# Attention's last batches and the second routing in another order, and the second pair's loads directly behind the first's

## The reference

```
x = x + 0.5 * ffn(layernorm(x))
x = x + attention(layernorm(x))      # 16 heads of 16 channels, softmax over 256 keys
x = x + 0.5 * ffn(layernorm(x))
```

## Time and profile before

| | us |
|---|---|
| median of 3 runs | 862.64 (858.92 to 864.11) |
| the profiled execution | 856.83 |
| its span, first to last instruction | 855.1 |
| TensorE busy | 729.3 (85%) |
| VectorE busy | 602.2 (70%) |
| ScalarE busy | 432.6 (51%) |
| POOL busy | 458.0 (54%) |
| mean granted TensorE clock | 0.957 of full |

### The profile page before, as it was taken

One profiled execution on the slowest core, in us unless ns is written; L12 is line 12 of the kernel. 1 busy time (PEld: TensorE's weight loads), 2 busy tenths in 40 slices (PEclk: granted clock), 3 DMA queues, 4 the chain that ended last, 5 costly groups with the idle time before them and its releaser, 6 DMA issues.

```text
span 855.1 us, 17528 instructions
## 1 busy us (share of the span) xinstructions
PE 729.3 (85%) x4774; PEld 568.2 (66%) x4774; DVE 602.2 (70%) x1435; ACT 432.6 (51%) x922; POOL 458.0 (54%) x446
## 2 busy tenths in 40 slices
PE   1775649999999997789999889787499999999984
PEld 1443326788888886667766667555268888888872
DVE  4775737777777776477787577457387777777766
ACT  3655324555555555257656455454325555555551
POOL 6876723666666667433344342146516666666672
PEclk9999999999999999999999798689689999999998
DMA  8998878868888753544453223027555787887766
GB/s 303 347 388 333 314 238 319 282 217 281 266 284 294 242 192 117 188 158 162 148 184 120 92 106 121 34 68 262 201 162 184 252 256 258 268 268 242 228 229 227
DMA packets 87419, 188.87 MB, mean 221 GB/s; under 512 B 13072, under 2 KB 37920, under 8 KB 85792
## 3 DMA queue, kind: packets, MB, share of 16 engines
q1 hardware_dynamic: 47104, 106.07, 36.4%
q10 hardware_dynamic: 26448, 41.92, 14.8%
q0 software_dynamic: 13776, 39.75, 12.2%
HBM read 105.46 MB, written 65.45 MB: 200 GB/s over the span
## 4 chain that ended last, share of the span: by engine, by line
PE 35%; DVE 13%; another core or an unknown queue 4%; issue 3%; ACT 2%; POOL 1%; DMA 0%; SPq 0%; DVEq 0%; ACTq 0%
PE s_psT L945 12%; PE s_psG L969 6%; DVE s_a_nm L1732 4%; PE s_psO L1499 3%; PE s_psS L1464 2%; PE s_psS L926 2%; PE s_psS L912 2%; PE s_psG L1436 2%; PE s_psT L1480 1%; DVE all_x L2188 1%; PE s_psT L1484 1%; PE s_psR L1571 1%; PE s_psG L1449 1%; PE s_psG L1522 1%
## 5 line engine op out<-in xcount | busy, mean ns | idle before, releaser
L1357 POOL DMA_INDIRECT rows<-s_a_row,s_a_slot_i x64 | 62.4, 975 | 107.6 <-DVE s_a_slot_i L1860 88.9
L1132 POOL DMA_INDIRECT kbuf<-s_e_own_ys,s_e_own_place x79 | 80.9, 1024 | 66.3 <-ACT s_e_own_ys L1078 58.3
L1132 POOL DMA_INDIRECT kbuf<-f_e_ys,f_e_place x79 | 80.9, 1024 | 66.3 <-ACT f_e_ys L1078 58.6
L945 PE MATMUL f_bank<-f_e_w,f_e_th 128*128 x316 | 114.3, 462 | 2.0 <-ACT f_e_th L1100 1.9
L945 PE MATMUL s_psT<-s_e_own_w,s_e_own_th 128*128 x316 | 112.1, 455 | 1.9 <-SPq L811 0.9
L1732 DVE TENSOR_REDUCE s_a_nm<-s_psS 128x4 f32<-128x1024 f32 x64 | 78.3, 1223 | 50.1 <-PE s_psS L1464 40.5
L1999 ACT ACTIVATE s_a_pT<-s_psT 128x1024 f32<-128x1024 f32 x62 | 63.4, 1022 | 47.0 <-PE s_psT L1484 30.4
L1008 DVE TENSOR_TENSOR s_e_own_hb<-s_psT,s_e_own_bias 128x512 f32<-128x512 f32 x79 | 54.5, 690 | 39.7 <-PE s_psT L945 38.7
L1008 DVE TENSOR_TENSOR f_e_hb<-f_bank,f_e_bias 128x512 f32<-128x512 f32 x79 | 54.5, 690 | 39.1 <-PE f_bank L945 37.2
L603 POOL DMA_INDIRECT rows<-f_r_row,f_r_slot_i x64 | 66.5, 1039 | 27.0 <-issue 18.5
L945 PEld LDWEIGHTS f_bank<-f_e_w,f_e_th 128*128 128x128 f32 x316 | 60.5, 192 | 22.5 <-issue 3.7
(11 more groups left out here) (383 smaller groups left out, 1887.5 us busy)
## 6 DMA issues: line engine op xcount, KB each, us to landing
w_split<-stage ACTq DMA_DIRECT2D x10, 1536.0 KB
f_e_w<-w_split SPq DMA_DIRECT2D x24, 512.0 KB
s_e_own_w<-w_split SPq DMA_DIRECT2D x24, 512.0 KB
f_e_tb<-rows ACTq DMA_DIRECT2D x80, 144.0 KB
s_e_tb<-rows ACTq DMA_DIRECT2D x80, 144.0 KB
stage<-w_raw SPq DMA_DIRECT2D x11, 768.0 KB
s_a_qs<-s_a_qk SPq DMA_DIRECT2D x32, 256.0 KB, 2.5
s_a_ks<-s_a_qk SPq DMA_DIRECT2D x30, 256.0 KB, 2.5
```

The lines of the kernel that those rows point to most:

```text
L945: last = pe.matmul(psH[j][:, :], left[:, p % 2, j, k * P:(k + 1) * P], w1[:, bass.ds(buf, 1), h, k * I2:(k + 1) * I2], start=n == 0, stop= ...
L1132: pool.indirect_dma_start(out=kbuf[:, :], out_offset=bass.IndirectOffsetOnAxis(ap=place[:, n:n + 1], axis=0), in_=ys[:, n, :], in_offset=N ...
L1357: pool.indirect_dma_start(out=rows[:, :], out_offset=bass.IndirectOffsetOnAxis(ap=slot_i[i][:, t, k:k + 1], axis=0), in_=row[i][:, t, :], ...
```

## The change

It does three things. In the tails of attention it turns group 5's rows before anything else and brings its logits, ranks, choice and slots forward; it places batch 6's output product `result(b - 1)` between the last two scores and the one before, and group 6's shift, rows, turn and choice accordingly; POOL issues five of group 5's sends before group 6's root and three between the two roots. It gathers the fillers behind the last ranks: 18 before, 15 after. And in `experts`, in both layers, ScalarE issues pair 1's loads directly behind pair 0's, so before step -1 copies pair 0's turned rows.

```
@@ -1083,6 +1083,7 @@
                 split.high(act, e, (k,))
 
         fetch(0)
+        fetch(1)
         for s in range(-1, NP + 4):
             if pair(s - 4):
                 scaled(s - 4, 1)
@@ -1109,7 +1110,7 @@
                 if (s - 3) % (BANK // 2) == 0:
                     column.load((s - 3) // (BANK // 2))
                 scaled(s - 3, 0)
-            for p in range(1 if s == -1 else s + AHEADP, s + AHEADP + 1):
+            for p in range(2 if s == -1 else s + AHEADP, s + AHEADP + 1):
                 if pair(p):
                     fetch(p)
             high_parts(s, 1)
@@ -1374,11 +1375,10 @@
         cycle(step)
 
         send(B - 4, (6, 7))
-        send(B - 3, (0, 1))
+        send(B - 3, range(5))
         routed_root(B - 2)
-        send(B - 3, (2, 3))
+        send(B - 3, (5, 6, 7))
         routed_root(B - 1)
-        send(B - 3, (4, 5, 6, 7))
         send(B - 2, range(8))
         for g in range(B - 2):
             routed.landed(pool, g)
@@ -1647,41 +1647,39 @@
         cycle(step)
 
         b = B - 1
+        rows_turned(b - 2)
         maxima(b, 1)
         scores_by_key(b, 3)
         by_dim(b - 1, 1)
-        rows_turned(b - 2)
+        logits(b - 2)
         scores_by_key(b, 4)
         values(b, 1)
+        ranks(b - 2)
         scores_by_key(b, 5)
         by_query(b, 0)
+        result(b - 1)
         scores_by_key(b, 6)
         scores_by_key(b, 7)
-        logits(b - 2)
         values(b, 2)
         by_dim(b, 0)
         values(b, 3)
-        ranks(b - 2)
+        gates_turned(b - 2)
         by_query(b, 1)
-        result(b - 1)
+        rows_turned(b - 1)
         by_dim(b, 1)
-        gates_turned(b - 2)
-        fill(2)
+        logits(b - 1)
+        fill(1)
         result(b)
         biases(b - 2)
-        rows_turned(b - 1)
-        fill(1)
-        logits(b - 1)
+        ranks(b - 1)
         fill(2)
         rows_turned(b)
-        ranks(b - 1)
+        gates_turned(b - 1)
         logits(b)
         fill(4)
         ranks(b)
-        gates_turned(b - 1)
-        fill(4)
         biases(b - 1)
-        fill(5)
+        fill(8)
         pe.wait_ge(s_r["cols"], 1)
         tile_turns(pe, c, tiles, psO).then_inc(s_r["line"], 1)
         gates_turned(b)
@@ -1917,24 +1915,24 @@
         b = B - 1
         routed_turned(b - 2)
         attended_low(b - 1, 1)
-        normalise(b, 0)
         routed_choice(b - 2)
-        attended_low(b, 0)
         routed_order(b - 2)
         routed_weights(b - 2)
         routed_slots(b - 2)
-        normalise(b, 1)
+        normalise(b, 0)
         add(b - 1)
         routed_stats(b - 1)
+        attended_low(b, 0)
+        routed_shift(b - 1)
+        normalise(b, 1)
         attended_low(b, 1)
-        routed_shift(b - 1)
+        routed_choice(b - 1)
+        routed_order(b - 1)
         add(b)
         routed_stats(b)
-        routed_shift(b)
-        routed_choice(b - 1)
-        routed_order(b - 1)
         routed_weights(b - 1)
         routed_slots(b - 1)
+        routed_shift(b)
         routed_biases(b - 2)
         routed_choice(b)
         routed_order(b)
@@ -2110,22 +2108,22 @@
         maxima(b, 1)
         exponentials(b, 3)
         attended_high(b - 1, 1)
+        routed_residual(b - 2)
         exponentials(b, 4)
-        routed_residual(b - 2)
+        routed_exp(b - 2)
         keep_values(b, 1)
         exponentials(b, 5)
         exponentials(b, 6)
         exponentials(b, 7)
         keep_values(b, 2)
         attended_high(b, 0)
-        routed_exp(b - 2)
+        routed_norm(b - 1)
         keep_values(b, 3)
+        routed_gates(b - 2)
+        routed_turned(b - 1)
         attended_high(b, 1)
-        routed_gates(b - 2)
-        routed_norm(b - 1)
-        routed_turned(b - 1)
+        routed_exp(b - 1)
         routed_norm(b)
-        routed_exp(b - 1)
         routed_turned(b)
         routed_exp(b)
         routed_residual(b - 1)
```

7 lines of the change are left out of this document (2 added, 5 removed).

## The result

The changed kernel took 866.11 us (median of 20 runs, 863.93 to 868.4), the kernel before beside it 864.08 us (20 runs, 855.63 to 866.11): a ratio of 1.0048, 95% interval 1.003 to 1.0067. The ratios are not those of the medians, which here lie only 2.0 us apart, and they leave out executions more than 1.5% above the fastest of their kernel, two of e7_first's twelve. By the two ratios the change costs some 4 to 6 us, half a per cent: within the forecast range and within 1%, but more than the +0.8 us forecast, and clear of zero.

What follows compares the result with a forecast made beforehand. The prediction took POOL's line of sends, and behind it group 7's slots, to bound the stretch from attention's end to the second layer's first expert tile; +0.6 (sends) +0.1 (first layer) +0.1 (held) on 862.64 gave 863.4 us, range 857 to 869.

Steps and rivals of the forecast that it cites:

- held results: Attention's last turns beside group 5's five sends: results possibly seen late, 0 to +1 us, taken as +0.1.
- the tail: Fewer fillers beside VectorE's table, which is seen when the sends end: costed at nothing, bounds 0 to +1 us.
- Group 5 first: End of attention: group 5's choice starts 5.2 us sooner, its first send at 575.5 instead of 581.11, 5.6 us sooner.
- POOL's new order: Five sends instead of two before group 6's root: root at 582.9 instead of 584.5, 1.6 of 5.6 us left.
- What waits behind that root: ScalarE's copy of batch 7's last values waits for group 6's root; batch 7's last turn 5.8 us later.
- The output product of batch 7: End of attention on TensorE: product done at 589.6 against 585.46, 4.1 us later.
- rival C: TensorE's clock: fewer fillers, lower level in the first expert tile, +2.6 us, giving 865.2 us; chance 0.1.
- Rival B: Group 7's logits held until group 6's run of sends ends: sends end 4.5 us later, 867.1 us; chance 0.2.
- the sign that I had named for it: VectorE waiting 4 us and more for group 7's logits was to show Rival B.
- Theory P: From e6_pause, not the prediction: table columns slow for another reason, such as padding rows' transfers; 5 us or more slower.
- The loads: Second pair's earlier loads on ScalarE's queue: nothing gained, some 4 us of cover; first layer 0 to 1 us, taken 0.1.
- I am wrong if results of TensorE are not held: If not held in runs of sends, group 7's slots come at about 604; end 1 to 2 us forward with POOL.

Runs made afterwards that it cites:

- e7_first: Kernel before, with POOL waiting behind the first two of group 6's sends until group 7's slots are there: 855.33 us, ratio 0.9916 to the kernel before.
- e4_copy: Changed kernel with ScalarE's group 6 rows behind its copy of batch 7's last values, VectorE's group 6 shift behind batch 7's second normalisation: 871.65 us, ratio 1.0134.
- e8_fill: Changed kernel with the fillers of the kernel before: 867.02 us, ratio 1.0067 to the kernel before.
- e6_pause: Changed kernel with POOL waiting, ahead of group 7's eight sends, until VectorE has done the table's columns: 862.74 us, ratio 1.0019 to the kernel before.
- e12_loads: e7_first with the second pair's loads directly behind the first's: 816.98 us, ratio 1.0059 to the kernel before.
- e9_three: Kernel before, with POOL waiting for group 7's slots behind three of group 6's sends: 812.15 us, ratio 1.0002 to the kernel before.
- e10_op: Kernel before, with one root-like POOL operation into a spare tile between group 6's fourth and fifth sends: 813.6 us, ratio 1.0029.
- e1_loads: Kernel before, with only the second pair's loads moved directly behind the first's: 863.01 us, ratio 1.003 to the kernel before.

## Why the prediction was right, and where not

The range was right, and so was the likeliest case in outline: the lead of group 5 was lost before group 6's sends. But the lead went to a held increment more than to the wait for the root that I had put first (e4_copy), and two terms that I had put at next to nothing, held results and the tail, were the large ones; that the sum stayed inside the range is in part luck. The size was wrong: +0.8 forecast, +4 to +6 measured. Step by step, behind G:

**Group 5 first.** Forecast 17.6 for its first send, measured 18.5. The choice began 13.7 us behind G, where I had 12.8, behind a subtraction that waited 3.52 us for ScalarE; the 4.5 us to the slots were right.

**POOL's new order.** Root 6 was to be 1.6 us sooner; it was 1.1 sooner.

**What waits behind that root.** ScalarE's copy did follow group 6's rows directly, at 587.99. But e4_copy shows that the order isn't the cause: taken away, the copy waits for the values' increment. The term that failed is "Held results, bounded": "0 to +1; I take 0.1, as the root's wait covers most". The row for it, group 5's turn held for 2.5 us, stood in my own, and I had taken five more sends beside attention's last values as covered. They held one increment for 3.9 us behind the last pass's end (5.7 in e4_copy).

**The output product of batch 7**: forecast to be done 31.7 behind G, measured 36.5. Of the 4.8 us, 1.6 are the later turn, 1.7 that four more steps took 5.0 us between turn and product where I had 3.4, and 1.4 the product at half clock, which I had priced only for the expert tiles (rival C), where nothing was lost: 1.20 us for the first four passes, before 1.19. Group 6's sends, forecast 36.7, came at 41.0.

**Rival B**, the logits held to the run's end, did not come, although the sign that I had named for it did: VectorE waited over 4 us for group 7's logits.

```profile
605.83 0.19 DVE L1808 TENSOR_TENSOR s_a_logit<-s_psT,all_gate_b 128x32 f32<-128x32 f32 x1 [4.16 <-PE s_psT L1571]
```

They were themselves late, through TensorE at 605.8, and taken at once, so the sign did not tell a held result from a late one. Nor were the ranks held to the run's end, as the forecast itself had it. They were issued at 609.3, behind seven sends, and seen at 610.24. The end of the sends was forecast at 58.5 and came at 61.6, near rival B's 62.4 but by the late start of group 6.

**The tail** is the other step that failed: "They lie beside VectorE's table; the table is seen when the sends end, so I cost them at nothing", with bounds 0 to +1. I asked whether the fillers were hidden, and they were (e8_fill). I had seen TensorE's results held, and never asked it of VectorE, which waits for its own semaphore between the table's dependent operations. Before, these ran at the start of group 7's run, behind a pause of 2.04 us, and were free; now group 7's sends follow group 6's 0.6 us after and the table meets a run that is already long. +3.0 us in the tail. Theory P had another candidate: the Trainium skill, "GPSIMD Engine Reference", "8. Key points", says that GpSimd shares its SBUF interfaces with VectorE, with contention where a VectorE instruction is in a 2-port mode or has two SBUF inputs. The trace speaks against it here: a column operation with two inputs (L294) took 0.16 us beside the sends of the changed kernel and 0.16 without them in e6_pause; only the gaps grew.

**The loads** cost nothing, as forecast, under the cover that I named ("some 4 us before it costs anything"); e12_loads shows the price when it is gone.

**What I'd have needed:** the same reading for every engine. As for "I am wrong if results of TensorE are not held": they are held on the chips of the first two series and in the profile that I started from; on the chip of the last series they are not, and the prices of this forecast don't apply there.

## What to carry to other kernels

Where a long line of indirect sends stands beside chains of small dependent operations, look at the gaps between these, not at their durations: gaps as long as the sends' spacing were the mark of late semaphore increments here, on the engine's own chain too. A pause for the sending engine just where such a chain starts can pay more than it costs (e6_pause, e7_first), and an engine that starts sooner pays nothing if its run then covers the next chain. Measure on more than one chip before such a cure is kept: e7_first gained 0.7 to 0.8% where the increments are late, and its near twin e9_three nothing where they are not.

## What the runs showed of the hardware

The runs differ in this by the chip, and the kernel's time with them: 861 to 864 us in the result's runs and the first two series, 811 us on the chip of the last, for the same kernel. That chip was measured in one series only, so something else about this series could be the reason. On the slower ones increments of TensorE and VectorE come late, by up to 9.5 us, while GpSimd issues indirect DMAs back to back and for up to 3 us after; on the faster one neither count found any, in the same run of twenty sends. VectorE's own chain was never stretched before the ninth send of a run. For TensorE's results how long a run must be isn't settled: batch 7's values were held from the fourth send on, beside loads at 320 GB/s. What makes a chip do one or the other isn't known from these runs, nor that the 50 us are all due to it; TensorE's granted clock in attention's cycle differs too (0.85 and 1.00), and which follows from which was not tested. Whether an ordinary GpSimd operation lets the increments through was not answered (e10_op ran on the chip that holds nothing); in the changed kernel's trace two came through just behind group 6's root, at 585.66 and 585.70.

The execution-to-execution scatter of the kernel before (10.5 us in the result's runs, the changed one 4.5) may be the same thing: by its two traces with that POOL order, before and e1_loads, the table's turns are held in one and not in the other, and the second tile's turn lies 3.8 us further behind G where they are held. That is argued from two executions, not shown.
